# A perceiver layer on one core: gain and bias of the latents applied as columns, three tiles centered by another engine, Pool's round in another order

## The reference, cut to what matters

```python
def _L0_xattn_ref(x, latents, mask, ln_x_g, ln_x_b, ln_l_g, ln_l_b, qn_g, kn_g, Wq, Wkv, Wout, bout):
    xn = layernorm(x, ln_x_g, ln_x_b)              # the context: 2 x 1024 rows of 256
    ln = layernorm(latents, ln_l_g, ln_l_b)        # 2 x 64 rows of 256
    q = (ln @ Wq).reshape(b, m, h, d).transpose(0, 2, 1, 3)
    kv = jnp.concatenate([xn @ Wkv, ln @ Wkv], axis=1)
    k, v = ...                                     # 16 heads of 64; keys and values of context and latents
    qn = rmsnorm(q, qn_g) * scale
    kn = rmsnorm(k, kn_g)
    attn = softmax(where(mask, qn @ kn^T, -max))
    return (attn @ v) @ Wout + bout
...
x = x + _L0_xattn_ref(ctx_1024, _layernorm(x), mask, ...)
x = x + _L0_attn_ref(_layernorm(x), ...)           # self attention over the batch dimension
x = x + _L0_ffn_ref(_layernorm(x), ...)            # a small mixture network
```

## Time and profile before

| | us |
|---|---|
| median of 3 executions | 237.33 (237.19 to 237.52) |
| the profiled execution | 236.85 |
| its span, first to last instruction | 235.1 |
| TensorE busy | 222.3 (95%) |
| VectorE busy | 155.3 (66%) |
| ScalarE busy | 151.2 (64%) |
| Pool busy | 80.4 (34%) |

### The profile page before, as it was taken

One profiled execution on the slowest core, in us unless ns is written; L12 is line 12 of the kernel. 1 busy time (PEld: TensorE's weight loads), 2 busy tenths in 40 slices (PEclk: granted clock), 3 DMA queues, 4 the chain that ended last, 5 costly groups with the idle time before them and its releaser, 6 DMA issues.

```text
span 235.1 us, 4158 instructions
## 1 busy us (share of the span) xinstructions
PE 222.3 (95%) x1449; PEld 191.7 (82%) x1449; DVE 155.3 (66%) x351; ACT 151.2 (64%) x331; POOL 80.4 (34%) x126
## 2 busy tenths in 40 slices
PE   7598999999999999999999999999999999899884
PEld 7264887786798889898888979899999988899773
DVE  1779999998878877768577655666766752304441
ACT  4245579797886768695857477787877765414251
POOL 5368866774384636473441500000000010000200
PEclk9799999999999999999999999999999999999999
DMA  6975110100000000000000699800000000000000
GB/s 170 298 228 220 37 34 25 45 22 25 0 25 0 0 3 3 0 0 3 0 0 3 199 395 352 223 0 3 1 3 0 0 4 0 0 3 0 0 3 22
DMA packets 11236, 13.80 MB, mean 59 GB/s; under 512 B 1584, under 2 KB 9936, under 8 KB 10960
## 3 DMA queue, kind: packets, MB, share of 16 engines
q1 hardware_dynamic: 10944, 13.01, 17.7%
q10 hardware_dynamic: 272, 0.52, 0.7%
HBM read 13.14 MB, written 0.13 MB: 56 GB/s over the span
## 4 chain that ended last, share of the span: by engine, by line
PE 68%; DVE 16%; ACT 4%; issue 4%; DMA 3%; POOL 3%; SPq 1%; ACTq 0%; DVEq 0%; POOLq 0%
PE banks L1193 19%; PE banks L1060 14%; PE banks L1107 9%; PE banks L1136 8%; PE banks L1326 5%; DVE small L803 4%; DMA rows<-in_L_xattn_ln_x_b 3%; PE banks L1207 3%; DVE sk L815 3%; PE banks L1138 2%; PE banks L1247 2%; PE banks L1353 1%; DVE raw L771 1%; DVE small L810 1%; ACT sk L533 1%
## 5 line engine op out<-in xcount | busy, mean ns | idle before, releaser
L838 DVE TENSOR_TENSOR ptl<-banks,pth 128x512 fp32r<-128x512 f32 (+1 forms) x48 | 26.8, 558 | 24.1 <-ACT pth L586 23.1
L1193 PE MATMUL banks<-xnh,pth 128*128 128x256 f32 x128 | 37.6, 294 | 0.0
L1193 PE MATMUL banks<-xnh,ptl 128*128 128x256 f32 x128 | 36.3, 283 | 0.0
L1193 PE MATMUL banks<-xnl,pth 128*128 128x256 f32 x128 | 36.2, 283 | 0.0
L586 ACT ACTIVATE pth<-banks 128x512 fp32r<-128x512 f32 (+1 forms) x48 | 23.7, 494 | 10.5 <-PE banks L1060 9.4
L533 ACT ACTIVATE sk<-banks 128x512 f32<-128x512 f32 x36 | 20.6, 606 | 14.2 <-PE banks L1107 14.1
L468 POOL TENSOR_TENSOR small<-small 128x16 f32<-128x16 f32 x7 | 20.4, 2909 | 27.3 <-DVE small L810 27.3
L815 DVE TENSOR_TENSOR sk<-banks,small 128x512 f32<-128x512 f32 x36 | 23.0, 679 | 6.9 <-POOL small L468 6.9
L803 DVE TENSOR_REDUCE small<-sk 128x8 f32<-128x512 f32 x36 | 23.6, 679 | 5.3 <-ACT sk L533 5.1
L449 POOL COPY sp<-sp 128x64 f32<-128x64 f32 x16 | 4.1, 254 | 62.8 <-ACT sp L567 62.8
L1193 PEld LDWEIGHTS banks<-xnh,pth 128*128 128x128 f32 x128 | 24.5, 192 | 0.4 <-issue 0.4
(11 more groups left out here) (183 smaller groups left out, 478.1 us busy)
## 6 DMA issues: line engine op xcount, KB each, us to landing
knT<-in_L_attn_qkv_kernel SPq DMA_DIRECT2D x1, 3072.0 KB, 12.2
raw<-in_ctx SPq DMA_DIRECT2D x16, 128.0 KB, 2.0
knT<-in_L_xattn_Wq SPq DMA_DIRECT2D x1, 1024.0 KB, 8.9
wv<-in_L_xattn_Wkv SPq DMA_DIRECT2D x1, 1024.0 KB, 5.2
wout_sb<-in_L_xattn_Wout SPq DMA_DIRECT2D x1, 1024.0 KB, 5.3
knT<-in_L_attn_out_kernel SPq DMA_DIRECT2D x1, 1024.0 KB, 15.0
wraw<-in_L_xattn_Wkv ACTq DMA_DIRECT2D x1, 512.0 KB, 4.0
wraw<-in_L_xattn_Wkv SPq DMA_DIRECT2D x1, 512.0 KB, 6.2
```

The source lines that it names most:

```text
L838: nc.vector.tensor_tensor(ptl[:, j0:j1, :], banks[:, t3_bank(u, c), 0:(j1 - j0) * P].rearrange("p (j r) -> p j r", j=j1 - j0), pth[:, j0:j ...
L1193: nc.tensor.matmul(banks[:, u_bank(u), 0:D], p_[:, j, :], x_, start=(j == 0 and i == 0), stop=False)
```

## The change

- Gains and biases of the two layer norms come in a second time, as 8 rows of 128 numbers (`gb8`), two rows each by four small loads, two on SP's queue and two on ScalarE's. TensorE transposes them once into 8 columns (`gcols`).
- The latents (n = 0) and context tile 0 (n = 1) are transposed when only centered and scaled; gain and bias are applied by ScalarE as scale and bias of each partition where the transposes leave their bank (`scaled`, two pieces of 128 columns), once as the high part and once in full (`lnTf`, `x0Tf`); `xt_low` reads the full copy.
- The rows ln_l_g, ln_l_b are loaded behind tile 3 instead of first, and Pool makes the latents in rows (`lnf`) in its round 4. The block with the four copies and Wv moves from behind tile 4 to behind tile 8, and ScalarE's conversion of the copies (`lnhl`) from round 3 to round 8. Pool's product of the query gains moves from round 0 to 3.
- SP loads tile 1 ahead of the rows ln_x_g, ln_x_b, and tile 2 ahead of Wq; Wk's second half stays behind tile 0.
- Tiles 1 to 3 are centered by ScalarE with scale and bias (1/deviation, and minus mean times that, a third small operation in Pool's `tile_rstd`).
- Pool's round becomes: product with ln_x_g, low part of the tile before, deviation of the next tile, sum with ln_x_b. Before it was product, sum, deviation, low part.
- TensorE: 9 warm-up products instead of 10, 4 more behind the first transposes; in the latents' second half the order of two passes is exchanged. VectorE: `xt_low` ahead of the centering of tile 0, statistics of tiles 3 to 5 in other places.

```diff
@@ sync
-            sp.dma_start(gl, row(ln_l_g)).then_inc(w_lrows, 16)
-            sp.dma_start(bl, row(ln_l_b)).then_inc(w_lrows, 16)
+            for i, v in enumerate((ln_l_g, ln_l_b)):
+                sp.dma_start(*gain_rows(i, v)).then_inc(w_cols, 16)
             for k in range(B * NT):
                 if k >= 4:
                     sp.wait_ge(xn_ready, k - 3)
+                if k == 4:
+                    sp.wait_ge(xt_ps, 2)
                 sp.dma_start(raw[:, k % 4, :], ctx_tiles[k]).then_inc(w_ctx[k % 4], 16)
                 if k == 0:
                     sp.dma_start(wraw[:, :, 512:1024], wkv_v[:, :, 512:1024]).then_inc(w_k[1], 16)
+                if k == 1:
                     sp.dma_start(rows[:, 0, :], row(ln_x_g)).then_inc(w_rows, 16)
                     sp.dma_start(rows[:, 1, :], row(ln_x_b)).then_inc(w_rows, 16)
-                if k == 1:
+                if k == 2:
                     sp.dma_start(wq_sb, wq_v).then_inc(w_q, 16)
                 if k == 3:
+                    sp.dma_start(gl, row(ln_l_g)).then_inc(w_lrows, 16)
+                    sp.dma_start(bl, row(ln_l_b)).then_inc(w_lrows, 16)
...
-                if k == 4:
+                if k == 8:
                     sp.wait_ge(ln_ready, 1)
                     for b in range(B):
                         for half in range(2):
@@ gpsimd
+                if centered_by_act(k):
+                    link(last)
+                    last = nc.gpsimd.tensor_scalar(nmr[:, k % 4:k % 4 + 1], mv[:, k % 4, 0:1], -1.0, rstd[:, k % 4:k % 4 + 1],
+                                                   ALU.mult, ALU.mult)
+                last.then_inc(rstd_ready, 1)
...
                 if i + 1 < B * NT:
-                    tile_norm(i + 1)
+                    norm_scale(i + 1)
+                if 0 < i <= B * NT:
+                    context_low(i - 1)
                 if i + 2 < B * NT:
                     tile_rstd(i + 2)
-                if i < B * NT:
-                    context_low(i)
-                if i == 0:
+                if i + 1 < B * NT:
+                    norm_shift(i + 1)
+                if i == 4:
+                    pool.wait_ge(lat_hat, 1)
+                    pool.wait_ge(w_lrows, 32)
+                    link(nc.gpsimd.tensor_tensor(lmul, latg, gl, ALU.mult))
+                    nc.gpsimd.tensor_tensor(lnf, lmul, bl, ALU.add).then_inc(ln_ready, 1)
+                if i == 3:
@@ scalar
+            def tile_center(k):
+                act.wait_ge(rstd_ready, k + 1)
+                nc.scalar.activation(raw[:, k % 4, :], raw[:, k % 4, :], ACT.Identity, bias=nmr[:, k % 4:k % 4 + 1],
+                                     scale=rstd[:, k % 4:k % 4 + 1]).then_inc(xhat_ready, 1)
+            def scaled(dst, n):
+                for c in range(DC):
+                    g = 2 * DC * n + c
+                    last = nc.scalar.activation(dst[:, c, :], banks[:, t1_bank(n), c * P:(c + 1) * P], ACT.Identity,
+                                                bias=gcols[:, g + DC:g + DC + 1], scale=gcols[:, g:g + 1])
+                return last
...
             wk_high(0)
-            xt_high(0)
-            nc.scalar.activation(lnTf, ...)
+            act.wait_ge(cols_ps, 1)
+            nc.scalar.activation(gcols, banks[:, 6, 0:4 * DC], ACT.Copy).then_inc(cols_ready, 1)
+            act.wait_ge(cols_ready, 1)
+            act.wait_ge(xt_ps, 1)
+            scaled(xth[:, 0], 0).then_inc(xth_ready, 1)
+            scaled(lnTf, 0).then_inc(lnT_ready, 1)
             wk_high(1)
             squares(0, 0)
-            xt_high(1)
+            act.wait_ge(xt_ps, 2)
+            scaled(xth[:, 1], 1).then_inc(xth_ready, 1)
+            scaled(x0Tf, 1).then_inc(x0T_ready, 1)
             squares(0, 1)
+            tile_center(1)
             context_high(0)
...
-                if i == 3:
+                if i == 8:
                     act.wait_ge(w_lat, 16 * 2 * B)
                     nc.scalar.activation(lnhl[:, :, :], lat2, ACT.Copy).then_inc(lnh_ready, 1)
@@ vector
-            dve.wait_ge(w_lrows, 32)
-            nc.vector.scalar_tensor_tensor(latg, xb[:, :], lmv[:, 0:1], gl, ALU.subtract, ALU.mult).then_inc(lat_hat, 1)
-            dve.wait_ge(lat_hat, 1)
             dve.wait_ge(lat_rs, 1)
-            nc.vector.scalar_tensor_tensor(lnf, latg, lrs, bl, ALU.mult, ALU.add).then_inc(ln_ready, 1)
+            center(latg, xb[:, :], lmv[:, 0:1], lrs).then_inc(lat_hat, 1)
...
-            keep_clock(10, 7)
+            keep_clock(9, 3)
+            pe.wait_ge(w_cols, 64)
+            nc.tensor.transpose(banks[:, 6, 0:4 * DC], gb8, ident[0:4 * DC, 0:4 * DC]).then_inc(cols_ps, 1)
             norm_transposed(0)
+            keep_clock(4, 3)
```

More of the change, by code:

```diff
@@ L113, in perceiver_layer @@
         gl = early(4, 0, D)
+        gb8 = early(2, 0, P)[0:8, :]
+        lmul = early(2, D, D)
+        x0Tf = early(2, 2 * D, D).rearrange("p (c r) -> p c r", c=DC)
         bl = early(4, D, D)
@@ L142, in perceiver_layer @@
         mcol = small[:, 202:203]
+        gcols = small[:, 204:212]
+        nmr = small[:, 212:216]
         b0keys = knT[:, 0, :, :].rearrange("p g n -> p (g n)")
@@ L435, in tile_norm, with norm_shift @@
                     pool.wait_ge(w_rows, 32)
-                link(nc.gpsimd.tensor_tensor(xg[:, :], raw[:, k % 4, :], rows[:, 0, :], ALU.mult))
+                else:
+                    pool.wait_ge(xn_ready, k)
+                own[0] += 1
+                scaled_at[k] = own[0]
+                nc.gpsimd.tensor_tensor(xg[:, :], raw[:, k % 4, :], rows[:, 0, :], ALU.mult).then_inc(pchain, 1)
+            def norm_shift(k):
+                pool.wait_ge(pchain, scaled_at[k])
                 if k >= 2:
                     pool.wait_ge(xt_ps, k)
+                    pool.wait_ge(xnl_ready, k - 1)
                 nc.gpsimd.tensor_tensor(xn[:, k % 2, :], xg[:, :], rows[:, 1, :], ALU.add).then_inc(xn_ready, 1)
@@ L510, in _ @@
             act.dma_start(wraw[:, :, 0:512], wkv_v[:, :, 0:512]).then_inc(w_k[0], 16)
+            for i, v in enumerate((ln_x_g, ln_x_b)):
+                act.dma_start(*gain_rows(2 + i, v)).then_inc(w_cols, 16)
             def xt_high(n):
@@ L880, in _ @@
             xt_low(1)
-            tile_center(1)
             key_norm2(0, 1)
@@ L1098, in project @@
                     pe.wait_ge(wk_hi, h + 1)
-                for k, (a, w) in enumerate(((xth, wkh), (xth, wkl), (xtl, wkh))):
-                    if k == 1 and i == 0:
+                order = ((xth, wkh), (xth, wkl), (xtl, wkh))
+                if i == 0 and h == 1:
+                    order = ((xth, wkh), (xtl, wkh), (xth, wkl))
+                for k, (a, w) in enumerate(order):
+                    if i == 0 and w is wkl:
                         if h == 1:
```

60 lines of the change are left out of this document (39 added, 21 removed).

## The result

The changed kernel takes 241.97 us (median of 4 runs, 240.95 to 243.07) against 237.43 (237.19 to 237.53): a ratio of 1.020, 95% interval 1.0174 to 1.0226. It is slower, as forecast, but by 4.5 us where the forecast had 0.7 and its range ended at 239.6. The profiled execution took 242.44, span 240.7. Its busy time, in the page's first part, has hardly moved against the earlier trace rows: ScalarE 4 us more, VectorE 2.4 less, TensorE 2.2 more.

A forecast was written before the change was run, and what follows sets the result against it. It took TensorE, busy 95% of the span, as the bound. Keys +0.15, clock +1.3 and later rounds -0.7 gave +0.75 on 236.85: 237.6 us for a profile, 238.0 for the median, range 235.4 to 239.6.

The forecast's parts named there:

- The front: Work up to item 3's products: 3.4 us won there, then given back at tile 9's load, keys +0.15.
- the rows don't come earlier: Rival, chance 0.08: ln_x_b still lands near 11, tile 5's centering ends 1.2 later, 239.2 us.
- The chain from tile 5's centering to the keys: From 26.9, Pool's latents, SP's block and tile 9's late load bring TensorE its keys at 40.1.
- The clock: After TensorE's pause from about 36.0 to 40.1 the clock falls to 0.50: +1.3 us, at most 1.7.
- Two falls at two places: Rival, chance 0.24: the clock also falls in TensorE's wait for tile 1, 13.9 to 15.5: +1.0, 239.0 us.
- Later rounds: Fewer Pool and VectorE collisions and the latents' conversion leaving round 3: -0.7 us, bounds 0 and 1.0.
- No stall: Rival, chance 0.12: tile 9 doesn't queue behind Wv, lands about 36.3, the clock holds: 233.8 us.

The follow-up runs named there:

- e9_rows_first: e8_block10_low_clock with the rows ln_x_g and ln_x_b issued ahead of the second half of Wk: 234.69 us.
- e1_block10: The changed kernel with the block of four latent copies and Wv behind tile 10 instead of tile 8: 235.19 us.
- e15_block8_front: The changed kernel with the ln_x rows ahead of Wk's second half and tile 1's sum ahead of tile 2's deviation on Pool: 240.44 us.
- e2_wv12: The changed kernel with Wv alone moved behind tile 12, the four copies staying behind tile 8: 236.73 us.
- e3_keepclock: The changed kernel with sixteen unused identity products filling TensorE's pause before item 5's key transposes: 239.3 us.
- e7_block10_lowpart: e1_block10 with Pool's low part of the latents made only after VectorE has scaled item 9's keys: 234.9 us.
- e8_block10_low_clock: e7_block10_lowpart with seven identity products in TensorE's first pause, ahead of tile 1's transposes: 234.14 us.
- e6_block10_oldpool: e1_block10 with Pool's round back in the old order, sum before deviation and low part: 235.51 us.
- e14_sum_first_nofill: e8_block10_low_clock with tile 1's sum ahead of tile 2's deviation on Pool, and without the seven filling products: 234.37 us.
- e4_before_block8: The kernel before with only its block of copies and Wv moved from behind tile 4 to behind tile 8: 239.29 us.
- e10_dve_centers: e8_block10_low_clock with the centering of tiles 1 to 3 back on VectorE instead of ScalarE: 234.84 us.
- e5_before_block8_conv8: The kernel before with the block moved behind tile 8 and ScalarE's conversion of the latents moved to round 8: 237.32 us.

## Why the prediction was right and wrong

From Pool's late latents on the mechanism was right: the block behind them, tile 9 behind Wv, VectorE standing 4.41 (forecast 4), TensorE standing 4.29 between 38.7 and 42.98 (forecast 4.1, 36.0 to 40.1), and the clock at 0.50 behind it. Taken against the profiled execution's 236.85, the sum was +0.75 and came out at 5.59. The step that failed most is the first: when the front lets Pool begin the latents in rows, and by which path.

**The front (forecast +0.15 at item 5's keys, measured +3.03).** Of the 2.88 between them, 2.1 is there when tile 5's centering ends: 28.96, where the forecast had 26.9 and as its worst bound 27.9. It is there already at tile 1's transposes, 17.61 for 15.5, by two terms of 1.4 and 0.65.

ln_x_b landed at 10.91, not 9.5; the chain of waits still names it first, against the earlier trace rows:

```profile
3.67 7.24 DMA rows<-in_L_xattn_ln_x_b
```

Two rows fewer ahead of it did not bring it forward: the second half of Wk, ahead of it in both kernels, was issued 0.35 earlier (2.21) and landed 0.34 later (9.10). With the same order of issue the profiled landings lie between 9.77 and 11.33. The forecast took 9.5, in the favourable half of its bounds, from the spacing of the latents' rows; the condition of the rival "the rows don't come earlier", at 0.08, came true here, but its 239.2 is 2.8 too low as well. e9_rows_first shows that order can move the landing: 6.82. It isn't the only gate. In e1_block10 the rows and Wk's second half both landed earlier, the rows at 9.77, and tile 1's transposes came 1.06 earlier (16.55). In e15_block8_front the rows alone went ahead (6.51), and Pool's product of tile 1 came only 0.5 earlier (14.32 for 14.85): there VectorE's statistics of tile 1 came last, behind the low part of Wk's second half. The forecast had no term for that half.

The second term is Pool's new order. Pool's timeline, after, and then the two lines of before:

```profile
11.05 0.98 POOL L469 TENSOR_TENSOR xg<-raw,rows 128x256 f32<-128x256 f32 x1 [2.71 <-DMA rows<-in_L_xattn_ln_x_b]
...
14.85 0.73 POOL L469 TENSOR_TENSOR xg<-raw,rows 128x256 f32<-128x256 f32 x1 [0.72 <-ACT raw L570]
15.67 0.19 POOL L447 TENSOR_SCALAR small<-small 128x1 f32<-128x1 f32 x1
15.94 0.55 POOL L448 TENSOR_TENSOR small<-small 128x1 f32<-128x1 f32 x1
16.60 0.27 POOL L455 TENSOR_SCALAR small<-small 128x1 f32<-128x1 f32 x1
16.83 0.73 POOL L476 TENSOR_TENSOR xn<-xg,rows 128x256 f32<-128x256 f32 x1
```
```profile
15.24 0.74 POOL L436 TENSOR_TENSOR xg<-raw,rows 128x256 f32<-128x256 f32 x1 [0.86 <-DVE raw L771]
16.05 0.74 POOL L439 TENSOR_TENSOR xn<-xg,rows 128x256 f32<-128x256 f32 x1
```

Three operations for tile 2 stand between product and sum of tile 1. From landing to the end of that sum are 6.65 us after, 5.7 before (11.09 to 16.79). The forecast counted those three operations, "again about 1.0", and by adding durations and gaps got 6.0 in all. The old 5.7 plus the 1.16 that they take (15.67 to 16.83) would have been 6.9. It also set its 15.5 against 17.46, when TensorE took tile 1, and not against 16.79, when Pool had it; the sum goes on from 15.5 itself and isn't changed by that, but for Pool its own figures gave a gain of 1.3 and not of 2.0. The profiles with the new order have 6.5 to 6.8 from landing to transposes (the changed kernel, e1_block10, e2_wv12, e3_keepclock, e7_block10_lowpart, e8_block10_low_clock), those with the sum ahead of the deviation 5.3 (e6_block10_oldpool, e14_sum_first_nofill).

What item 3's products did win, 1.6, comes behind tile 1: without small waits TensorE needs 5.59 from those transposes to the products, where the earlier trace rows have 7.35. The forecast had 5.9 for it; that term held.

But from there the forecast took the wrong path. It let TensorE's products and VectorE's round set the time, "because Pool, no longer late, removes the small waits there too". In the changed kernel Pool stays last: between 13 and 34 us the chain of waits that ended last runs 16.2 us through Pool and 0.8 through VectorE, in the kernel before 4.8 and 10.6. TensorE's gain doesn't reach Pool, whose sum of tile 5 starts at 31.36, in the kernel before at 31.02. ScalarE's centering of tile 3 waits for Pool's deviation, and VectorE waits for the squares that stand behind it on ScalarE. ScalarE's, VectorE's and Pool's timelines:

```profile
21.30 0.60 ACT L570 ACTIVATE raw<-raw,small 128x256 f32<-128x256 f32 x1 [1.46 <-POOL small L455]
```
```profile
22.42 1.29 DVE L880 TENSOR_REDUCE small<-sk 128x8 f32<-128x512 f32 x2 [1.01 <-ACT sk L595]
```
```profile
28.66 0.34 POOL L528 TENSOR_SCALAR small<-small 128x1 f32<-128x1 f32 x1
29.04 0.74 POOL L469 TENSOR_TENSOR xg<-raw,rows 128x256 f32<-128x256 f32 x1
...
31.36 0.75 POOL L476 TENSOR_TENSOR xn<-xg,rows 128x256 f32<-128x256 f32 x1
```

The product of tile 5 (29.04) stands right behind the product of the query gains (28.38 to 29.00), which the change moved into this round. So by this trace even a centering done at 26.9 would have found Pool busy until 29.00.

**The chain from tile 5's centering to the keys (forecast 13.2, measured 14.02).** Pool 4.79 for 4.6; SP from the first copy to tile 9's issue 3.09 for 2.75 (the upper bound was 3.1); landing 5.0 for 4.9; statistics and half the scaling 1.1 for 1.0. All four misses were small and in the same direction. e2_wv12 put Wv's transfer at 2.6 of the landing, as the earlier trace rows had it.

**The clock (forecast +1.3, at most 1.7; measured 2.3 in the trace, 2.7 by e3_keepclock).** The keys are 3.03 late and the round start after next 5.32, so 2.29 fall in the stretch at 0.50. The direction was right; the length was taken from the one row at hand, 3.41, as a ceiling, and it was 6.83. It doesn't follow from the pause alone: in e4_before_block8 it was 6.83 too, behind a pause of 1.38. Two falls at two places, the rival at 0.24, did not come in this profile: the first pause passed at 1.00. That its 1.67 matches the forecast's 1.6 is luck, as both its ends came 2 us later (15.94 to 17.61 for 13.9 to 15.5). A fall there came in e2_wv12, around a pause of 2.38. Beside that rival stood a rule of the Trainium skill, TensorE: Matmul & The Clock Gate, Part 4: PE-mode transpose: transposes don't count as busy time in the way that products do. In this trace ten transposes stood behind the first pause (17.61 to 18.75), and the clock held. So it doesn't bear out what the forecast drew from the rule, and no run tells transposes from products.

**Later rounds (forecast -0.7, bounds 0 to -1.0; measured +0.27).** A gain from Pool's order shows, 0.9 between one profile each of e1_block10 and e6_block10_oldpool. But the conversion that left round 3 arrived in round 8, and its low part on Pool meets VectorE's clamp: 0.86 of TensorE's time (e7_block10_lowpart). The forecast counted the leaving and not the arriving. That the two cancel is argued from those runs; no run isolates it with the block behind tile 8.

Together: 2.88 + 0.99 + 0.97 = 4.84 more than the forecast's 0.75, which is 5.59. Every term of the sum erred to the same side, and the bounds themselves were too narrow: tile 5's centering (28.96 against 27.9 at worst), the clock (2.3 against 1.7) and the later rounds (+0.27 against 0) all came out beyond them.

"No stall" (233.8) failed in the changed kernel. Its condition came true in e1_block10, when the block moved out of the way, at 235.19, 1.4 above its figure. What stays open is how much of the 2.1 in the front each gate alone would give back, whether ScalarE's centering is worth anything (e10_dve_centers), and why the second half of Wk and ln_x_b did not land earlier with less ahead of them.

## What to carry to other kernels

When a step is made earlier, ask on which engine's rounds the next steps hang, and compare that engine with itself: here TensorE's products came 1.6 earlier, and Pool's sums no earlier at all. Price a reordered chain by its old length in the trace plus what is put into it (5.7 + 1.16, for a measured 6.65), not by a sum of durations (6.0). When a block on an in-order queue waits for a value, its place and the time of that value are one decision: the same block behind tile 8 cost nothing with early latents (e5_before_block8_conv8); with late ones the whole change came out 4.5 us slower there and 2.3 faster with the block behind tile 10. A work item that is moved away from a crowded round has to be costed where it arrives, too.

## What the runs showed of the hardware

The granted clock fell to 0.50 in a pause of 4.29 us and was there for 6.83 us, with TensorE busy for 5.80 of them. With pauses of 4.13 (e15_block8_front) and 2.38 (e2_wv12) it was 0.50 for 3.4; with 1.67, 1.65 and 2.11 (the changed kernel, e1_block10 and e7_block10_lowpart, at tile 1) it stayed at 1.00 in their profiles. But it also fell behind pauses of 1.80 (for 3.41) and 1.38 (e4_before_block8, for 6.83), so that in these traces the length of one pause doesn't decide. VectorE's clamp on 16 elements a partition took 0.17, and 0.95 to 1.06 while Pool subtracted 64x512 elements; both times it ended 0.03 to 0.04 behind Pool's operation (52.23 for 52.20 in e1_block10, 59.88 for 59.84 in the changed kernel). A load of 128 KB behind 1 MB on the same queue landed 4.5 to 5.0 after its issue, in sixteen profiles, and 2.4 after it in e2_wv12, without the 1 MB.
